# Row records turned on TensorE into a table in SBUF instead of loaded from HBM in 20-byte pieces, and places made into the selection matrix where they land

## The reference

```
h = (layernorm(x) @ W.T).reshape(n, 8, 32)
alpha = sum(h[src] * a_src) + sum(h[dst] * a_dst)            # per edge and head
alpha = alpha + sum(relu(edge_attr @ edge_W.T + edge_b).reshape(-1, 8, 32) * h[dst])
alpha = leaky_relu(alpha, 0.2)
attn = softmax of alpha over the edges of one dst
out = segment_sum(h[src] * attn, dst) + bias
x = x + out;  then  x = x + ffn(layernorm(x))
```

## Time and profile before

| | us |
|---|---|
| timed runs, median of 3 | 3159.52 (3158.77 to 3161.25) |
| profiled execution, its span from first to last instruction | 3570.8 |

### The profile page before, as it was taken

One profiled execution on the slowest core, in us unless ns is written; L12 is line 12 of the kernel. 1 busy time (PEld: TensorE's weight loads), 2 busy tenths in 40 slices (PEclk: granted clock), 3 DMA queues, 4 the chain that ended last, 5 costly groups with the idle time before them and its releaser, 6 DMA issues. The chain is left out here.

```text
span 3570.8 us, 36328 instructions
## 1 busy us (share of the span) xinstructions
PE 2454.9 (69%) x8642; PEld 1654.1 (46%) x8642; DVE 2278.8 (64%) x3546; ACT 1022.1 (29%) x2822; POOL 1909.1 (53%) x2041
## 2 busy tenths in 40 slices
PE   1657676677677777776766767777766554269998
PEld 1424444444444444444444444444444332168887
DVE  7957767676667777776667777766666554251223
ACT  3522222222222222222222222222223221043332
POOL 3656566566566666666666665666666452607000
PEclk9857777777777777777777777777777676559999
DMA  8355555556555555556555555556556993310000
GB/s 269 122 140 145 153 145 153 145 148 178 143 157 146 154 147 149 155 143 177 141 158 147 153 155 142 157 146 175 153 145 147 124 122 57 87 28 3 19 19 31
DMA packets 341609, 471.12 MB, mean 132 GB/s; under 512 B 115596, under 2 KB 262718, under 8 KB 341170
## 3 DMA queue, kind: packets, MB, share of 16 engines
q0 software_dynamic: 90000, 262.14, 30.9%
q1 hardware_dynamic: 250578, 206.73, 20.0%
q10 hardware_dynamic: 848, 0.26, 0.0%
HBM read 380.17 MB, written 88.72 MB: 131 GB/s over the span
## 5 line engine op out<-in xcount | busy, mean ns | idle before, releaser
L1005 POOL DMA_INDIRECT src_in<-t_node_rows,rec_in x1760 | 1685.2, 957 | 1134.7 <-issue 549.0
L1067 PE MATMUL p_sum<-weighted,hot 128*128 128x264 f32 x3520 | 1287.9, 529 | 588.1 <-issue 384.4
L1067 PEld LDWEIGHTS p_sum<-weighted,hot 128*128 128x128 f32 x3520 | 893.7, 264 | 954.5 <-issue 631.7
L1208 DVE SCALAR_TENSOR_TENSOR prod<-p_enc,near 128x512 f32<-128x512 f32 x880 | 563.3, 681 | 382.9 <-ACT near L1134 328.9
L1258 DVE TENSOR_TENSOR weighted<-src_in,p_turn 128x1024 f32<-128x1024 f32 x440 | 534.5, 1215 | 309.8 <-ACT p_turn L1142 119.0
L1212 DVE TENSOR_REDUCE dots<-prod 128x32 f32<-128x1024 f32 x440 | 536.9, 1220 | 15.2
L1045 PE MATMUL p_pick<-win,hotT 128*128 128x272 f32 x880 | 383.6, 524 | 136.0 <-ACT near L1134 51.5
L1155 ACT COPY sums<-p_sum 128x264 f32<-128x264 f32 x440 | 164.5, 374 | 908.8 <-issue 403.2
L1134 ACT COPY near<-p_pick 128x272 f32<-128x272 f32 x440 | 169.9, 386 | 734.4 <-remote 383.4
L1038 PE MATMUL p_enc<-expander,attrT 30*128 30x256 bf16 x1760 | 321.2, 310 | 48.1 <-DMA attrT<-t_block_attr 36.8
L1045 PEld LDWEIGHTS p_pick<-win,hotT 128*128 128x128 f32 x880 | 154.7, 220 | 249.3 <-issue 179.8
(11 more groups left out here) (334 smaller groups left out, 1674.1 us busy)
## 6 DMA issues: line engine op xcount, KB each, us to landing
win<-t_node_rows SPq DMA_DIRECT2D x440, 136.0 KB
t_block_sums<-sums SPq DMA_DIRECT2D x110, 528.0 KB
places<-t_block_places SPq DMA_DIRECT2D x110, 256.0 KB
src_in<-t_node_rows,rec_in POOLq DMA_INDIRECT x1760
attrT<-t_block_attr SPq DMA_DIRECT2D x330, 36.0 KB
t_node_rows<-out_rows SPq DMA_DIRECT2D x49, 136.0 KB, 1.7
x<-in_x SPq DMA_DIRECT2D x4, 1536.0 KB, 25.6
out_x<-x SPq DMA_DIRECT2D x48, 128.0 KB
```

The lines of the kernel that those rows point to most:

```text
L1005: pool.indirect_dma_start(src[:, q.par, b, k, :], None, scr["rows"], bass.IndirectOffsetOnAxis(ap=rec_i[:, q.s % ROWS_RING, b, k:k + 1], a ...
L1067: last = nc.tensor.matmul(p_sum[b % 2][:, 0:ROW], hot[:, q.par, b, :], weighted[:, b, k, :], start=(k == 0), stop=(k == W - 1))
L1208: nc.vector.scalar_tensor_tensor(prod[:, 2 * half:2 * half + 2, :], p_enc[(PAIRS * b + half) % len(p_enc)][:, :, :], 0.0, near[:, q.par, b ...
```

## The change

- `rec_in`, its load, its ring of semaphores and `block_rows` with its store go away.
- `ro` now lies as five planes of 128 rows (`[P, W+1, P]`), shared by prologue and loop. The sources are converted from integer to float by an added copy, so that TensorE can turn them.
- TensorE turns each plane by a 128x128 transpose (`turn_table`) into a free part of the bank `p_turn`, and VectorE copies it (`keep_turned`) into `row_src` or `row_near`, which hold two groups. The five planes of group 0 are done at the start of the loop; those of the next group one each in steps 19 to 23 of a group.
- `places` goes away: its transfer lands in `hotT`, and Abs and Relu work there in place. The transfer's wait is for `picked` now, and its place is behind the windows.
- The waits for `rec_in` on POOL and ACT are gone, but for one wait a group.

```diff
@@ make_rows_of
-    nc.vector.tensor_scalar(ro[:, :, 0:W].bitcast(I32), words.rearrange("p (r k) -> p r k", k=W), (1 << SRC_BITS) - 1, DUMMY,
-                            ALU.bitwise_and, ALU.bitwise_xor)
+    x.link(nc.vector.tensor_scalar(ro[:, 0:W, :].bitcast(I32), words.rearrange("p (r k) -> p k r", k=W), (1 << SRC_BITS) - 1, DUMMY,
+                                   ALU.bitwise_and, ALU.bitwise_xor))
...
+    x.wait()
+    nc.vector.tensor_copy(ro[:, 0:W, :], ro[:, 0:W, :].bitcast(I32))
...
-    nc.vector.tensor_scalar(ro[:, :, W], place, -1.0, 1.0, ALU.mult, ALU.add)
+    nc.vector.tensor_scalar(ro[:, W, :], place, -1.0, 1.0, ALU.mult, ALU.add)
@@ store_table
-    nc.sync.dma_start(scr["block_rows"][block, :], ro[0:n, :, :].rearrange("p r w -> p (r w)")).then_inc(stored, 16)
@@ load_places
-                    sp.wait_ge(s["hotT"], q.prev().s)
+                    sp.wait_ge(s["picked"], Q * q.prev().s)
...
-                sp.dma_start(places[:, q.par, :, :].rearrange("p q r -> p (q r)"), v.broadcast_to([P, Q * P])).then_inc(s_places[q.par], 16)
+                sp.dma_start(hotT[:, q.par, :, :].rearrange("p q r -> p (q r)"), v.broadcast_to([P, Q * P])).then_inc(s_places[q.par], 16)
@@ load
-                load_rows(q)
-                load_places(q)
                 load_attr(q)
                 load_windows(q)
+                load_places(q)
                 load_flags(q)
@@ gather
-                pool.wait_ge(s_rec[q.s % ROWS_RING], 16 * (q.s // ROWS_RING + 1))
-                nc.gpsimd.sem_inc(s["waited_by_pool"], 1)
+                group, first = divmod(q.s, turn)
+                if first == 0:
+                    pool.wait_ge(s["rows_turned"], (W + 1) * (group + 1))
+                    nc.gpsimd.sem_inc(s["waited_by_pool"], 1)
...
-                                                bass.IndirectOffsetOnAxis(ap=rec_i[:, q.s % ROWS_RING, b, k:k + 1], axis=0)
+                                                bass.IndirectOffsetOnAxis(ap=row_src[:, group % 2, k, at_block:at_block + 1], axis=0)
@@ tensor engine
+            def turn_table(group, k):
+
+                if group:
+                    pe.wait_ge(s["rows_out"], group)
+                if group or k:
+                    pe.wait_ge(s["rows_turned"], (W + 1) * group + k)
+                nc.tensor.transpose(p_turn[:, P:2 * P], ro[:, k, :], keep["ident"][:, :]).then_inc(s["rows_up"], 1)
+
...
+                group, u = divmod(q.s - RING, turn)
+                pe.wait_ge(s["row_top"], q.s + 1)
+                if 0 <= group < GROUPS - 1 and 0 <= u - TURNED_AT <= W:
+                    turn_table(group + 1, u - TURNED_AT)
                 turn_rows(q)
@@ make_hotT
-                if q.since(RING):
-                    act.wait_ge(s["picked"], Q * q.prev().s)
-                nc.scalar.activation(hotT[:, q.par, :, :].rearrange("p q r -> p (q r)"), of, ACT.Relu, scale=-1.0, bias=1.0).then_inc(s["hotT"], 1)
+                nc.scalar.activation(of, of, ACT.Relu, scale=-1.0, bias=1.0).then_inc(s["hotT"], 1)
@@ vector engine
+            def keep_turned(group, k):
+
+                dve.wait_ge(s["rows_up"], (W + 1) * group + k + 1)
+                turned_to = row_src[:, group % 2, k, :] if k < W else row_near[:, group % 2, :]
+                nc.vector.tensor_copy(turned_to, p_turn[:, P:2 * P]).then_inc(s["rows_turned"], 1)
```

More of the change, by code:

```diff
@@ L850, in edge_loop @@
         row_of = lambda v: v.rearrange("p (q h) -> p q h", q=Q)
-        s_rec = [m.sem(f"s_rec_loaded{i}") for i in range(ROWS_RING)]
         s_attr = [m.sem(f"s_attr_loaded{i}") for i in range(RING)]
@@ L884, in _ @@
         def _(sp):
-            def load_rows(q):
-                if q.s >= ROWS_RING:
-                    before = straight(q.s - ROWS_RING)
-                    for b in range(Q):
-                        sp.wait_ge(s_src[before.par][b], 16 * W * (before.turn + 1))
-                    sp.wait_ge(s["hot"], Q * (before.s + 1))
-                rows = scr["block_rows"].rearrange("(n q) (r w) -> n r q w", q=Q, w=W + 1)
-                v = rows[q.s, :, :, :] if isinstance(q.s, int) else rows[bass.ds(q.s, 1), :, :, :].rearrange("o r q w -> (o r) q w")
-                sp.dma_start(rec[:, q.s % ROWS_RING, :, :], v).then_inc(s_rec[q.s % ROWS_RING], 16)
             def load_attr(q):
@@ L1094, in last @@
                     add_up(straight(STEPS - 1), b)
+            for k in range(W + 1):
+                turn_table(0, k)
             for b in range(Q):
@@ L1390, in _ @@
             x = Chain(dve, s["moved"])
+            for k in range(W + 1):
+                keep_turned(0, k)
             for b in range(Q):
```

47 lines of the change are left out of this document (25 added, 22 removed).

## The result

| | median us | lowest to highest | runs |
|---|---|---|---|
| before | 3159.14 | 3157.46 to 3161.25 | 4 |
| after | 3084.07 | 3077.65 to 3084.61 | 4 |

The ratio is 0.9745, with a 95% interval of 0.972 to 0.977. The change makes the kernel 75 us faster; the prediction said 3160, with a range from 3132. Later runs took place on other chips, where the kernel before has medians of 3142 to 3151 us.

A forecast was written before the change was run, and what follows sets the result against it. The prediction took POOL's gather pace to bound the middle and transfers the last steps. Its terms, 4.9 + 0.5 + 1.5 + 0 + 0 - 6.0 = +0.9 us on 3159.5, gave 3160 us, range 3132 to 3176.

The forecast's parts named there:

- What bounds the kernel: Middle of the loop: bound by POOL's gather pace, 20.06 us a step, in an estimated timed step of 20.9 us.
- Places in the middle: Middle steps: places issued behind the windows still land with 8 us of cover in a timed step; 0.
- The 20-byte pieces: 512 pieces a step removed: hidden under POOL's pace in the middle, a gain only in the last steps.
- Rival B: Whole middle: transfers matter everywhere, so removing the pieces shortens each step; -30 us, 3130; chance 0.27.
- The start: Start of the loop: second places transfer issued 5.0 us later, so the second near comes later; +4.9 us, range 4 to 7.
- the prologue: Before the loop: an added 128x512 conversion stands ahead of the bases' store that the loop's start waits for; +0.5 us.
- Table making in the loop: Loop steps that unpack: three added conversions of 0.5 us on DVE, the longest engine there; +1.5 us (0 to 1.5).
- Turning the table: Loop: 15 transposes on PE and 15 copies on DVE, covered by POOL's work; 0, or 10 us with the cover gone.
- The end: Last eight steps: fewer pieces where transfers are the bound; -4.5 and -1.5 us, together -6.0, bounds 0 to -15.
- rival D: Start and end: the start costs and the end gives nothing, places landing last; +8 to +16 us, 3170; chance 0.20.
- Rival C: Middle steps: places come too late for ScalarE once the 8 us of cover are gone; +40 us, 3200; chance 0.08.

The follow-up runs named there:

- stand-in: Kernel before, with its row records read as 128 runs of 80 bytes instead of 512 pieces of 20: 3143.05 us, ratio 0.9996 to the kernel before.
- e7_order_only: Kernel before, with only the places load moved behind the windows, own buffer and wait kept: 3078.1 us, ratio 0.9803 to the kernel before.
- d1_spare_ahead: Changed kernel plus a second 256 KB places transfer each step to a spare tensor, first in the list: 3211.87 us, ratio 1.0211 to the kernel before.
- d2_spare_behind: Changed kernel plus a second 256 KB places transfer each step to a spare tensor, last in the list: 3090.78 us, ratio 0.9838 to the kernel before.
- h1_rows_last: Kernel before, with the row records' load moved from the front of the list to its end: 3199.42 us, ratio 1.0185 to the kernel before.
- h2_pieces_then_places: Changed kernel with places in front, and a transfer of 512 pieces of 20 bytes ahead of them: 3152.76 us, ratio 1.0014 to the kernel before.
- f1_start_ahead: Changed kernel with the first two steps' lists in the old order, places first: 3079.56 us, ratio 0.9771 to the kernel before.
- a_again: Changed kernel, unaltered, run again: 3083.74 us, ratio 0.9785 to the kernel before.
- e7_again: Kernel before with only places moved behind the windows, run a second time: 3076.5 us, ratio 0.9773 to the kernel before.
- e3_places_only: Kernel before with only the places part: loaded into hotT behind the windows, waiting for the picks: 3077.56 us, ratio 0.9786 to the kernel before.
- e5_places_first: Changed kernel with places first in each step's list again, still in hotT and waiting for the picks: 3203.44 us, ratio 1.0187 to the kernel before.

## Why the prediction was wrong, by its steps

- **What bounds the kernel.** POOL's pace was read rightly (the median distance of two gathers is 1.251 us in all later profiles). But "So I take the timed loop's middle as bound by POOL's pace" rested on 20.9 us a step, which came of putting the whole 411.3 us into the middle. Had part of it sat elsewhere, the step would have been longer, so 20.9 was a floor and was used as if it were the step. The stand-in has 21.29. Its stretches account for the difference: of the 424.9 us between the two spans (3570.8 less 3145.9), 370.8 lie in the middle (2521.5 less 2150.7) and 54.1 elsewhere. So a step lies 1.2 us above POOL's 20.06 in clean runs too.
- **Places in the middle: 0.** This is the step that failed. It asked when places are needed and found cover. That was right: ScalarE's Abs idles 0.0 us for them in the 101 steps after. It did not ask what the 256 KB had been in the way of. The term was put at 0 and measures -0.75 us a step, 75.9 us in the 101 steps; `raw`'s wait alone falls by 0.82 a step. `e7_order_only` shows the move alone, `d1_spare_ahead`, `d2_spare_behind`, `h1_rows_last` and `h2_pieces_then_places` show the cause.
- **The row that was not followed, and that would not have helped.** The `raw` of a middle step was not read; the earlier trace rows has it at the end, idle for 14.34 us for its gathers, and there it was taken as a matter of the last steps only. But the profile before hides it in the middle:

```profile
L1220 DVE TENSOR_TENSOR raw<-dots,src_in 128x128 f32<-128x128 f32 x100 | 28.7, 287 | 75.9 <-issue 51.0 <-DMA src_in<-t_node_rows,rec_in 23.9
```

There `raw` waits for its gathers for 23.9 us in all, against 174.5 in the stand-in: with stalls elsewhere, DVE came to `raw` when the gathers had mostly landed. The signal was readable only in a clean profile.
- **The 20-byte pieces: 0 in the middle.** Right for the pieces themselves, by two runs. But "SP saves 0.4 us a step and nobody waits for it" holds only because places were moved away at the same time: with places in front, the same 0.4 us cost 52 to 62 us. Rival B got the sign of the result and not its mechanism: nothing that it would do was seen when pieces were put back. Its premise, that part of the middle's waiting hangs on landings, was right, and its transfer was the wrong one. It said against itself that POOL's pace does not know the pieces; what it lacked was that POOL's pace was not all. The Trainium skill (DMA: Bandwidth & Descriptors, Specifications) has transfers under 512 B handled by read-modify-write. No run here shows that mechanism, and in this kernel 512 of them a step cost nothing that can be told.
- **The start: +4.9, and +0.5 in the prologue.** Right within what profiles of different chips can tell: the first stretch starts 5.4 us later than in the stand-in and 4.4 later than in the profile before. `f1_start_ahead` gives the order's part alone: 4.9 us.

```profile
183.29 4.24 SPq L911 DMA_DIRECT2D win<-t_node_rows  x4
...
190.60 3.71 SPq L911 DMA_DIRECT2D win<-t_node_rows  x4
...
194.35 0.43 SPq L904 DMA_DIRECT2D hotT<-t_block_places  x1
...
197.73 0.72 ACT L1127 ACTIVATE hotT<-hotT,after_p 128x512 f32<-128x512 f32 x1 [4.57 <-DMA hotT<-t_block_places]
...
199.02 0.37 ACT L1138 COPY near<-p_pick 128x272 f32<-128x272 f32 x1
...
200.20 0.95 POOL L997 DMA_INDIRECT src_in<-t_node_rows,row_src  x1 [9.69 <-ACT near L1138]
```

The timeline of the start after, against the earlier trace rows, has the windows at 183.29 (predicted 183.27), the second windows at 190.60 (190.7), the second places at 194.35 (194.4), `near` at 199.02 (199.7). The landing took 3.38 us in place of 4.06, the one term of this sum that was clearly off. The prologue's added conversion takes the 0.43 us that was expected, and the unpacking itself 0.62 in place of 0.43; no run shows how much of it reaches the start of the loop.
- **Table making in the loop: +1.5.** Not separated. The three added conversions take 0.43 us each and the three unpackings 0.61 in place of 0.42, so the work is there. What of it lengthens a step can't be told beside the 75.9 us.
- **Turning the table: 0.** Right within what the runs can tell: the kernels with and without it, `a_again` and `e7_again`, are 7.2 us apart with ranges that overlap. The fifteen copies in the middle have no idle time before them:

```profile
L1337 DVE CAST row_src<-p_turn 128x128 int32<-128x128 f32 x12 | 3.4, 283 | 0.0
L1337 DVE COPY row_near<-p_turn 128x128 f32<-128x128 f32 x3 | 0.8, 283 | 0.0
```

- **The end: -6.** Not borne out. The eight steps take 241.4 us after and 235.8 in the stand-in. Over the 15 later profiles they take 235.5 to 248.9, and no less with places behind than with places ahead, so single profiles tell little here. Two rows of a late step show what rival D said, places the last to land:

```profile
2504.78 0.72 ACT L1127 ACTIVATE hotT<-hotT,after_p 128x512 f32<-128x512 f32 x1 [12.95 <-DMA hotT<-t_block_places]
...
2506.26 1.25 PE L1037 MATMUL p_pick<-win,hotT 128*128 128x272 f32 x2 [12.26 <-ACT hotT L1129]
```

The pick is idle 12.26 us, less than the 18.50 of the earlier trace rows, but now for places, and the steps are no shorter for it. In `a_again`, a second profile of the same kernel, the Abs of that step waits 5.11 us in place of 12.95, so the size of this wait is not a constant.
- **Rival C** had the right transfer and the wrong side of it. Places behind the windows and the picks are not late; places ahead of them are what costs.

## What to carry to other kernels

When a transfer is moved, ask two questions: who waits for it, and what was waiting beside it. Here the moved 256 KB landed 15.5 us ahead of their use in the old place and 9.8 us in the new one (medians), and their old place, right beside the last gather of a step, cost 0.75 us in each of 101 steps. Whoever shortens such a list by half a microsecond moves everything behind it, and can lose more than the shortening was worth. Look for the landing that a step's length depends on, measure from the issue of that transfer to the first instruction that needs it, and count whose bytes move in between. The mean share of the transfer engines over the stretch says nothing of it, and their share in that moment does not either. Idle time of that instruction is a weaker sign, since it also hangs on when its engine is ready. And where a profile is longer than its timed runs, get a clean one of an equal kernel before working in differences.

## What the runs showed of the hardware that was not expected

- The profile before is 411 us longer than its timed runs; all 15 profiles taken since, of kernels that differ from it in as little as the order of two lines, agree with their timed runs to 11 us. So the stalls that it shows do not belong to the kernel's timed runs. What made them is open. The 20-byte pieces did not: `e3_places_only`, `e7_order_only` and `h1_rows_last` have them and clean profiles.
- One transfer of 256 KB a step costs 0 or 1.3 us by its place in one queue's list alone, and 0.5 us earlier or later changes a step by 0.4 to 0.6 us, at a mean transfer share of 0.61 to 0.67 in the middle of these kernels. In the 2.8 us behind the last gather the share is 0.92 to 1.00 in all kernels of the table above, fast or slow; what differs is what is moved there.
- TensorE's mean granted clock goes down as the steps grow longer. The trace has only two levels, 1.2 and 2.4 GHz (0.5 and 1.0 of full speed), and the mean says how long each was granted: the lower one for 664 us of the middle in the changed kernel, 760 in the stand-in and 910 with places in front again. The means are 0.84 and 0.82 (above), and in `e5_places_first`:

```profile
212.60:2420.90 2208.30, 1690.04 (x5857) 1055.91 (x5857) 1791.59 (x2549) 719.83 (x2120) 1546.54 (x1619) 0.79 0.61 173
```

PE is busy 1690 us there and 1609 in the changed kernel for the same 5857 matmuls. So shorter steps come with faster matmuls. The waits for `row_top` do not order the clock by themselves (220.7 us at 0.82 in the stand-in, 223.2 at 0.79 in `e5_places_first`), and how much of the gain goes by way of the clock was not separated.
